# An expert's last 64 second-weight rows by a transfer of their own, nine weight buffers instead of ten

## The chip, the cores and the metric

One core of one Trainium2 chip. The metric is the device time of one execution, in microseconds (us), as a median over runs. All engines, queues and buffers named here are those of this one core.

## What is computed

One layer on 1024 rows of width 256: layer norm with a modulation, attention with 16 heads, a second modulated norm, and a mixture of experts. The second half matters here, cut from the reference:

```python
logits = x @ gate_w.T
weights, sel = top_k(softmax(logits), 4)          # 4 of 60 experts for each row
for each expert e:                                # w13_e: 352 x 256, w2_e: 256 x 176
    gu_e = x @ w13_e.T
    h = silu(gu_e[:, :176]) * gu_e[:, 176:]
    acc = acc + cw_e[:, None] * (h @ w2_e.T)
out = shared + sparse                             # shared: one expert of width 704 for all rows
```

Everything is float32, and the kernel keeps the experts' products in float32.

## The kernel before, in words

**Blocks and pairs.** The kernel sorts the 4 x 1024 choices into blocks of 128 rows. `blocks_of` plans 45 blocks for the 60 experts (the 30 with most rows have a block each, the 30 others share 15 blocks, two to a block with 64 rows each), and a 46th block takes an overflow. Blocks are worked in 23 pairs: pair q has the even block 2q and the odd block 2q+1. All 15 shared blocks are odd ones; their pairs are 1, 2, 4, 5, 7, 8, 10, 11, 13, 14, 16, 17, 19, 20 and 21. So the pattern from pair 3 to pair 20 repeats every three pairs: one pair with two experts, two with three, 8 experts in all. The end differs a little: pair 21 also has three experts, and pair 22 has one and the overflow.

**Weights of an expert.** One row of `in_w` for each of 128 partitions: 2 x 352 values of the first weights, 256 values of the second weights' first 112 rows (`OWN`, on partitions 0 to 111), and 128 values more for the last 64 rows (`REST`): partitions 0 to 63 hold their output columns 0 to 127, partitions 64 to 127 hold columns 128 to 255. That is 1088 values or 4352 B on each partition, 544 KB, in one transfer that SP issues (`load`, L349 to L354) to slot k % 10 of the tile `w` (`RING` = 10). Before it issues load k, SP reads the expert's number (`value_load`) and waits until the block of load k-10 is finished (semaphore `m_y`).

**TensorE's order in pair q** (loop at L1609 and on), with e = 2q: `gate_up` of the even block (x times the first weights, L1567), the first turn of `down_rest` for the two blocks of pair q-2 (L1598), the transposes of rows for the next even block (`rows_of`, L1549), the transposes of the hidden values of pair q-1 (`hidden_T`, L1575 and L1576), the second turn of `down_rest` for pair q-2, `gate_up` of the odd block, `rows_of` again, and `down_own` for pair q-1 (L1582). A `gate_up` waits for all loads of its block and for the rows that ScalarE scales and shifts out of PSUM (`rows_T`, L746, semaphore `m_xtev`).

**The two turns of `down_rest`.** The 64 last hidden values of the even block lie on partitions 0 to 63 and those of the odd block on 64 to 127. In turn 0 each block multiplies its own half of the partitions, which gives one half of the 256 output columns. For the other half of the columns the weights lie on the other partitions, so VectorE copies the hidden values a second time with the halves exchanged (L1106, two copies of 64 x 128 in each pair), and turn 1 uses those. The two blocks' products go to PSUM banks PV and M. Turn 1 waits for turn 0 (`m_half`), and its end raises `m_y`, once for each block.

**VectorE in a pair:** the copies of `hidden_T` (L1106, L1107, L1108), the product of the even block (L1113), the two results of pair q-2 out of PSUM (`result`, L1123, raises `m_yev`, for which `down_own` and GpSimd's scatter wait), the product of the odd block (L1115, L1116). GpSimd issues indirect transfers: gathers of rows (L522), scatters of results (L527). At the end SP reads the scattered results back (L379), and VectorE and GpSimd add them up (L1158, L566).

Of the kernel before, what the change touches and what calls it, by code (L numbers as in the profile page):

```python
# [32 lines left out]
def adaln_layer(nc, x_in, cos_in, sin_in, c_in, wmod_in, wqkv_in, wo_in, wr_in, segu_in, sedn_in,  # L33
                w_in, plan_in, h2rows, ychoice, out):
# [3 lines left out]
    S, D = x_in.shape  # L38
    P = 128
# [16 lines left out]
    I = (w_in.shape[2] - D - D // 2) // (2 * NC)  # L56
# [9 lines left out]
    W_OWN, W_REST = NC * I13, NC * I13 + D  # L66
    WL = W_REST + D // 2
# [14 lines left out]
    RING = 10  # L82
    BUFS = RING
# [31 lines left out]
    with ctx:  # L115
# [34 lines left out]
        w = sb("w", [P, RING, WL])  # L150
# [26 lines left out]
        slotk = sb("slotk", [P, NT * TOPK])  # L177
        row = sb("row", [P, NT * TOPK])
        blk = sb("blk", [P, NT * TOPK])
# [42 lines left out]
        HS, HST = carve(P, 2 * I, 2), carve(P, 4 * P, 2)  # L222
# [27 lines left out]
        ld_w = [sem(f"ld_w{r}") for r in range(RING)]  # L250

        ld_plan, s_plan, s_count, s_look, s_route, m_half = (sem(n) for n in ("ld_plan", "s_plan", "s_count", "s_look", "s_route", "m_half"))
# [72 lines left out]
        def _(sp):  # L325
# [30 lines left out]
            def overflow_weights(b, done):  # L356

                x = sp.value_load(ovei[0:1, bass.ds(b, 1)], min_val=0, max_val=NE - 1)
                sp.dma_start(w[:, 0, :], w_in[bass.ds(x, 1), :, :].rearrange("e p n -> p (e n)")).then_inc(done, 16)
# [5 lines left out]
            sp.wait_ge(m_y, BLOCK_OF[NE - RING] + 1)  # L365
            overflow_weights(0, ld_w[0])

            nov = sp.value_load(novi[0:1, 0:1], min_val=1, max_val=MAXOV)
            with sp.If(nov > 1):
                with sp.Fori(1, nov) as b:  # L370
                    sp.wait_ge(m_yev, b + (NBLK - 1))
                    overflow_weights(b, o_ld)
# [410 lines left out]
        def _(dve):  # L783
# [395 lines left out]
        def _(pe):  # L1179
# [372 lines left out]
            def lanes_of(e):  # L1552
# [3 lines left out]
                return [(k % RING, k // RING + 1, n * i, n) for i, k in enumerate(held)]  # L1556

            alone = [(0, 0, 0, P)]
# [26 lines left out]
            def down_rest(turn, y1, b, blocks):  # L1585
# [136 lines left out]
```

## Time and profile before

| what | us |
|---|---|
| median of 3 runs | 483.09 |
| lowest and highest of the runs | 478.96 and 483.27 |
| the profiled execution's own time | 482.59 |
| its span, first to last instruction | 480.8 |
| mean granted clock of TensorE | 0.954 of full |

The profiled execution's own time is 1.8 us more than its span. Sums below are made against 482.59. The profile names tiles by what shares their memory: QS stands for most of the experts' working buffers, EP, PV and M for PSUM banks, w for the weight ring.

### The profile page before, as it was taken

How to read it: one execution, taken by the hardware profiler on the slowest of the kernel's cores; microseconds unless marked ns; L12 is line 12 of the kernel's file. 1: busy time of each engine (PE TensorE's matmuls, PEld its weight loads, DVE VectorE, ACT ScalarE, POOL GpSimd, SP SyncE). 2: the span in 40 equal slices, each digit the busy share in tenths (PEclk: the TensorE clock that was granted, in tenths of full speed). 3: DMA queues.
4: the chain of work that ended last, by engine and by line, in shares of the span. 5: the costliest groups of instructions: out<-in, count | busy, mean ns of one | idle time of the engine just before them, and what ended most of it. 6: DMA issues, size and time to landing. Idle time of an engine off the chain costs nothing.

```text
span 480.8 us, 7951 instructions
## 1 busy us (share of the span) xinstructions
PE 441.4 (92%) x2866; PEld 214.8 (45%) x2866; DVE 315.2 (66%) x710; ACT 252.1 (52%) x398; POOL 171.5 (36%) x194
## 2 busy tenths in 40 slices
PE   7988999999999999999999699989999999999870
PEld 4554523333333333333566467645555545554450
DVE  7478679999898999953188893534444444444284
ACT  1567657888888888887634132243333333332150
POOL 2058400202032120201010064786565665543343
PEclk8897769999999999999999889999999999999995
DMA  8500000000000000000110661248998998892281
GB/s 270 191 2 1 1 1 1 1 1 2 0 1 1 1 1 2 1 1 0 45 44 1 204 262 41 75 113 280 311 333 299 300 319 286 298 310 90 81 324 55
DMA packets 20530, 54.73 MB, mean 114 GB/s; under 512 B 4513, under 2 KB 8825, under 8 KB 20491
## 3 DMA queue, kind: packets, MB, share of 16 engines
q1 hardware_dynamic: 16075, 45.81, 27.9%
q0 software_dynamic: 4416, 8.41, 5.3%
q8 instruction: 23, 0.38, 0.3%
q14 instruction: 16, 0.13, 0.1%
HBM read 49.74 MB, written 8.13 MB: 120 GB/s over the span
## 4 chain that ended last, share of the span: by engine, by line
PE 75%; DVE 12%; ACT 5%; issue 4%; DMA 3%; SPq 1%; POOL 1%; POOLq 0%; DVEq 0%; ACTq 0%
PE EP L1567 13%; PE PV L1336 13%; PE M L1289 9%; PE EP L1323 6%; PE EP L1326 6%; PE EP L1426 4%; PE EP L1549 3%; PE PV L1582 3%; PE M L1582 3%; PE M L1503 2%; DMA w<-ychoice 2%; PE PV L1598 2%; DVE mx L871 2%; ACT QS L746 2%; PE EP L1254 2%
## 5 line engine op out<-in xcount | busy, mean ns | idle before, releaser
L871 DVE TENSOR_REDUCE mx<-M 128x1 f32<-128x512 f32 x256 | 159.5, 684 | 17.3 <-PE M L1289 17.2
L691 ACT ACTIVATE QS<-EP 128x1024 f32<-128x1024 f32 x128 | 124.1, 1022 | 30.0 <-PE EP L1326 29.6
L1567 PE MATMUL EP<-w,QS 128*128 128x352 f32 (+1 forms) x244 | 65.5, 477 | 5.4 <-ACT QS L746 3.7
L1336 PE MATMUL PV<-QS,VA 128*32 128x512 f32 x512 | 69.0, 612 | 0.0
L1289 PE MATMUL M<-KT,QT 64*128 64x512 bf16 x256 | 61.1, 406 | 3.3 <-DVE mx L871 2.9
L1106 DVE COPY QS<-M 64x128 f32<-64x128 f32 x46 | 13.3, 289 | 70.9 <-PE M L1576 70.6
L741 ACT ACTIVATE OT<-EP 128x176 f32<-128x176 f32 x46 | 14.6, 317 | 74.8 <-PE EP L1567 74.8
L1323 PE MATMUL EP<-QT,KT 64*128 64x512 bf16 x256 | 50.4, 385 | 0.4 <-ACT QS L691 0.2
L1326 PE MATMUL EP<-QTB,xh 34*128 34x512 bf16 x256 | 50.3, 385 | 0.0
L1289 PEld LDWEIGHTS M<-KT,QT 64*128 64x128 bf16 x256 | 18.3, 94 | 66.0 <-DVE mx L871 54.7
L1426 PE MATMUL EP<-segu,QSB 128*128 128x352 f32 x128 | 41.2, 465 | 2.8 <-DVE wide L945 2.8
L746 ACT ACTIVATE QS<-EP,modc 128x128 f32<-128x128 f32 x92 | 37.0, 454 | 10.0 <-PE EP L1549 9.4
L1567 PEld LDWEIGHTS EP<-w,QS 128*128 128x128 f32 (+1 forms) x244 | 28.4, 163 | 29.7 <-issue 12.7
L441 POOL TENSOR_TENSOR rsum<-OT,minus 128x16 f32<-128x16 f32 x6 | 17.5, 2909 | 57.7 <-ACT OT L652 57.7
L527 POOL DMA_INDIRECT ychoice<-xh,tab x26 | 25.7, 987 | 27.9 <-PE EP L1549 12.4
L522 POOL DMA_INDIRECT QS<-h2rows,tab x26 | 28.1, 1082 | 12.6 <-issue 7.6
L1426 PEld LDWEIGHTS EP<-segu,QSB 128*128 128x128 f32 x128 | 23.1, 190 | 15.3 <-issue 3.6
L430 POOL CAST QSB<-negm 128x16 bf16<-128x16 f32 x8 | 2.1, 266 | 69.3 <-DVE negm L880 69.3
L527 POOL DMA_INDIRECT ychoice<-QS,tab x20 | 19.8, 992 | 19.5 <-DVE QS L1123 10.5
L522 POOL DMA_INDIRECT qkv<-h2rows,tab x20 | 20.4, 1022 | 6.1 <-issue 6.1
L1598 PE MATMUL PV<-w,QS 64*64 64x128 f32 (+1 forms) x152 | 20.8, 300 | 0.0
L1598 PE MATMUL M<-w,QS 64*64 64x128 f32 (+1 forms) x152 | 20.8, 300 | 0.0
(277 smaller groups left out, 633.0 us busy)
## 6 DMA issues: line engine op xcount, KB each, us to landing
w<-in_w SPq DMA_DIRECT2D x61, 544.0 KB, 5.6
w<-ychoice SPq DMA_DIRECT2D x8, 512.0 KB, 7.6
segu<-in_segu SPq DMA_DIRECT2D x1, 1408.0 KB, 10.3
x<-in_x SPq DMA_DIRECT2D x2, 512.0 KB, 5.2
wide<-in_wmod SPq DMA_DIRECT2D x1, 1024.0 KB, 7.9
h2rows<-qkv SPq DMA_DIRECT2D x2, 512.0 KB, 3.9
out<-x SPq DMA_DIRECT2D x8, 128.0 KB, 1.8
sedn<-in_sedn SPq DMA_DIRECT2D x1, 640.0 KB, 10.5
```

The costliest lines, as they stand in the source:

```text
L522: pool.indirect_dma_start(out=XG[b], out_offset=None, in_=h2rows, in_offset=bass.IndirectOffsetOnAxis(ap=tab[:, 0, e:e + 1], axis=0), boun ...
L527: pool.indirect_dma_start(out=ychoice, out_offset=bass.IndirectOffsetOnAxis(ap=tab[:, 1, e:e + 1], axis=0), in_=YS[b], in_offset=None, bou ...
L691: nc.scalar.activation(PT[n % 3][:, 2 * p:2 * p + 2, :], EP[p][:, :, :], ACT.Exp, scale=HD ** -0.5).then_inc(e_done, 1)
L746: ins = nc.scalar.activation(XGT[b][:, c * P:(c + 1) * P], BANK[2 + b][:, c * P:(c + 1) * P], ACT.Identity, scale=modc[:, 4, c:c + 1], bia ...
L871: nc.vector.tensor_reduce(out=mx[:, u % 2, q, j, c:c + 1], in_=src, axis=AX.X, op=ALU.max).then_inc(m_free, 1)
L1289: mm(fill(m_free), QT[rows, 2 * g + j // 2, q0:q0 + P], KT[rows, g, 512 * c:512 * c + 512], start=True, stop=True).then_inc(m_fill, 1)
L1323: mm(EP[p][:, i, :], KT[rows, g, keys], QT[rows, 2 * g + p, queries], start=True, stop=False)
L1326: ins = mm(EP[p][:, i, :], KTB[rows, g, keys], QTB[rows, u % 2, p, :], start=False, stop=True)
L1336: ins = mm(PV[HP * j:HP * j + HP, :], VA[:, tt, g, :], PT[n % 3][:, j, :], start=tt == 0, stop=tt == NT - 1)
L1426: ins = mm(EP[part][:, a, 0:SHH], h2T[:, c, t * P:(t + 1) * P], segu[:, c, o:o + SHH], start=c == 0, stop=c == NC - 1)
L1567: ins = mm(BANK[b][lo:lo + n, 0:I13], XGT[b][:, c * P + lo:c * P + lo + n], w[:, r, c * I13:(c + 1) * I13], start=c == 0, stop=c == NC - 1)
L1598: ins = mm(BANK[6 + i][lo:lo + n, cols], HST[b][part, (2 + turn) * P + lo:(2 + turn) * P + lo + n], w[part, r, W_REST:WL], start=False, st ...
```

## The change

- The 128 values for the last 64 rows leave `in_w`: a row has 960 values (3840 B), a transfer 480 KB.
- A new input `in_rest` holds these 64 rows of every expert with all 256 columns. A second transfer for each load brings 64 rows of 1024 B (64 KB) to partitions 0 to 63 for an even block and 64 to 127 for an odd one. Both transfers raise the same semaphore, so that waits count by 32.
- A slot of `w` grows from 1088 to 1216 values for each partition, and the ring has `WRING` = 9 slots: load k waits for the block of load k-9.
- `down_rest` has one turn: each block multiplies its 64 hidden values with all 256 columns. It stands where turn 1 stood. `m_half` goes.
- VectorE's two exchanged copies (L1106) go. `HST` shrinks from 4 to 3 parts, and three small tiles move into the space.

```diff
+    WRING = 9
...
-        w = sb("w", [P, RING, WL])
+        w = sb("w", [P, WRING, WL + D])
...
                 x = sp.value_load(order[0:1, LOADS[k]:LOADS[k] + 1], min_val=0, max_val=NE - 1)
-                if k >= RING:
-                    sp.wait_ge(m_y, BLOCK_OF[k - RING] + 1)
-                sp.dma_start(w[:, k % RING, :], w_in[bass.ds(x, 1), :, :].rearrange("e p n -> p (e n)")).then_inc(ld_w[k % RING], 16)
+                if k >= WRING:
+                    sp.wait_ge(m_y, BLOCK_OF[k - WRING] + 1)
+                weights(x, k % WRING, BLOCK_OF[k] % 2, ld_w[k % WRING])
+
+            def weights(x, r, half, done):
+                rest = slice(HALF * half, HALF * half + REST)
+                sp.dma_start(w[:, r, 0:WL], w_in[bass.ds(x, 1), :, :].rearrange("e p n -> p (e n)")).then_inc(done, 16)
+                sp.dma_start(w[rest, r, WL:WL + D], rest_in[bass.ds(x * REST, REST), :]).then_inc(done, 16)
...
-                for i in range(experts):
-                    here, there = slice(REST * i, REST * i + REST), slice(REST * (1 - i), REST * (1 - i) + REST)
-                    nc.vector.tensor_copy(HST[b][there, 3 * P:4 * P], H[here, 2 * P:3 * P])
...
-                        pe.wait_ge(ld_w[r], 16 * loads)
+                        pe.wait_ge(ld_w[r], 32 * loads)
...
-                    d = (i + turn) % 2
-                    part, cols = slice(HALF * d, HALF * d + HALF), slice(P * d, P * d + P)
+                    part = slice(HALF * i, HALF * i + REST)
                     for r, loads, lo, n in lanes:
-                        ins = mm(BANK[6 + i][lo:lo + n, cols], HST[b][part, (2 + turn) * P + lo:(2 + turn) * P + lo + n], w[part, r, W_REST:WL],
-                                 start=False, stop=turn == 1)
-                    ins.then_inc(m_y if turn else m_half, 1)
+                        ins = mm(BANK[6 + i][lo:lo + n, 0:D], HST[b][part, 2 * P + lo:2 * P + lo + n], w[part, r, WL:WL + D],
+                                 start=False, stop=True)
+                    ins.then_inc(m_y, 1)
...
                 gate_up(e + 1, 0, lanes_of(e))
-                if q >= 2:
-                    down_rest(0, e - 2, b, two(e - 4))
                 if q:
                     rows_of(e + 1)
                     hidden_T(e, 1 - b)
                 if q >= 2:
-                    down_rest(1, e - 2, b, two(e - 4))
+                    down_rest(b, two(e - 4))
...
             down_own(NBLK // 2, 1 - b, two(NBLK - 2))
-            down_rest(0, NBLK, 1 - b, two(NBLK - 2))
+            down_rest(1 - b, two(NBLK - 2))
             shared_half(EARLY, 1, 1).then_inc(s_up, 1)
-            down_rest(1, NBLK, 1 - b, two(NBLK - 2))
```

## Rows read from the trace of the kernel before

**Rows 1.** The page: busy time by engine, and the last-ended chain's shares.
```profile
PE 441.4 (92%) x2866; PEld 214.8 (45%) x2866; DVE 315.2 (66%) x710; ACT 252.1 (52%) x398; POOL 171.5 (36%) x194
...
PE 75%; DVE 12%; ACT 5%; issue 4%; DMA 3%; SPq 1%; POOL 1%; POOLq 0%; DVEq 0%; ACTq 0%
```

**Rows 2.** Busy time by stretch: three pairs, from one odd gate_up to another.
```profile
core 0: us, PE busy (x) PEld busy (x) DVE busy (x) ACT busy (x) POOL busy (x), PEclk, DMA share, GB/s
416.21:433.97 17.76, 17.23 (x109) 9.05 (x109) 7.54 (x28) 6.65 (x18) 6.93 (x7) 1.00 0.87 289
```

**Rows 3.** Timeline of TensorE, from an even gate_up to the next odd one.
```profile
365.80 1.45 PE L1567 MATMUL EP<-w,QS 128*128 128x352 f32 x4
367.18 0.33 PE L1598 MATMUL PV<-w,QS 64*64 64x128 f32 x2
...
367.56 0.44 PE L1549 MATMUL EP<-ident,QS 128*128 128x128 f32 x2
367.84 0.38 PE L1575 MATMUL M<-ident,QS 128*112 128x128 f32 x2
...
368.26 0.33 PE L1598 MATMUL PV<-w,QS 64*64 64x128 f32 x2
368.27 0.33 PE L1598 MATMUL M<-w,QS 64*64 64x128 f32 x2
368.42 0.28 PE L1598 MATMUL PV<-w,QS 64*64 64x128 f32 x2
...
368.90 0.52 PE L1567 MATMUL EP<-w,QS 128*64 128x352 f32 x2 [0.19 <-ACT QS L746]
```

**Rows 4.** Timeline of ScalarE in the same stretch.
```profile
368.04 0.81 ACT L746 ACTIVATE QS<-EP,modc 128x128 f32<-128x128 f32 x2 [0.43 <-PE EP L1549]
```

**Rows 5.** SP's waits.
```profile
SPq L354 <- PE M L1598: 94.9, 19, 42.3
```

**Rows 6.** Timeline of the end of the last pair.
```profile
445.71 0.70 PE L1582 MATMUL PV<-w,QS 112*128 112x256 f32 x2 [0.22 <-DVE QS L1123]
...
446.77 0.37 PE L1598 MATMUL PV<-w,QS 64*128 64x128 f32 x1
...
447.38 0.98 POOL L527 DMA_INDIRECT ychoice<-QS,tab  x1 [0.31 <-issue]
...
448.79 0.27 PE L1598 MATMUL PV<-w,QS 64*128 64x128 f32 x1
...
449.10 0.42 DVE L1123 TENSOR_TENSOR xh<-PV,MOD 128x256 f32<-128x256 f32 x1 [3.44 <-PE M L1598]
...
450.30 0.97 POOL L527 DMA_INDIRECT ychoice<-xh,tab  x1 [1.94 <-DVE xh L1123]
```

**Rows 7.** Line L1106, VectorE's exchanged copies, over the whole span.
```profile
L1106 DVE COPY QS<-M x46: 283/289/294, 315.1 to 444.1; 64x128 f32<-64x128 f32 x46
```

**Rows 8.** Line L354, weight loads: two loads after the release at 416.
```profile
L354 SPq DMA_DIRECT2D w<-in_w x1: 341/341/341, 416.2 to 416.2; - x1
DMA to landing us min/median/max: 4.4/4.4/4.4
...
L354 SPq DMA_DIRECT2D w<-in_w x1: 333/333/333, 417.3 to 417.3; - x1
DMA to landing us min/median/max: 5.4/5.4/5.4
```

**Rows 9.** The same line at 368.9: first and second load after that release.
```profile
L354 SPq DMA_DIRECT2D w<-in_w x1: 342/342/342, 368.9 to 368.9; - x1
...
L354 SPq DMA_DIRECT2D w<-in_w x1: 333/333/333, 370.3 to 370.3; - x1
DMA to landing us min/median/max: 5.6/5.6/5.6
```

**Rows 10.** The page's DMA issues: KB of each, median us to landing.
```profile
w<-in_w SPq DMA_DIRECT2D x61, 544.0 KB, 5.6
...
out<-x SPq DMA_DIRECT2D x8, 128.0 KB, 1.8
```

More of the change, by code:

```diff
@@ L33, in adaln_layer @@
 def adaln_layer(nc, x_in, cos_in, sin_in, c_in, wmod_in, wqkv_in, wo_in, wr_in, segu_in, sedn_in,
-                w_in, plan_in, h2rows, ychoice, out):
+                w_in, rest_in, plan_in, h2rows, ychoice, out):
     f32, bf16, i32, u32 = mybir.dt.float32, mybir.dt.bfloat16, mybir.dt.int32, mybir.dt.uint32
@@ L221, in adaln_layer @@
         YS = carve(P, D, 4) + [xhf[:, D * b:D * b + D] for b in range(BUFS - 4)]
-        HS, HST = carve(P, 2 * I, 2), carve(P, 4 * P, 2)
+        HS, HST = carve(P, 2 * I, 2), carve(P, 3 * P, 2)
+        slotk, row, blk = carve(P, NT * TOPK, 3)
         SL = [OT[:, I * b:I * b + I] for b in range(2)]
@@ L249, in adaln_layer @@
         ld_qkv, ld_wo, ld_wr, ld_sh = sem("ld_qkv"), sem("ld_wo"), sem("ld_wr"), sem("ld_sh")
-        ld_w = [sem(f"ld_w{r}") for r in range(RING)]
-        ld_plan, s_plan, s_count, s_look, s_route, m_half = (sem(n) for n in ("ld_plan", "s_plan", "s_count", "s_look", "s_route", "m_half"))
+        ld_w = [sem(f"ld_w{r}") for r in range(WRING)]
+        ld_plan, s_plan, s_count, s_look, s_route = (sem(n) for n in ("ld_plan", "s_plan", "s_count", "s_look", "s_route"))
         s_eq, s_one, s_lo, s_hi, s_cells, s_read, s_tab = (sem(n) for n in ("s_eq", "s_one", "s_lo", "s_hi", "s_cells", "s_read", "s_tab"))
@@ L364, in _ @@
             sp.wait_ge(s_over, 1)
-            sp.wait_ge(m_y, BLOCK_OF[NE - RING] + 1)
-            overflow_weights(0, ld_w[0])
+            sp.wait_ge(m_y, BLOCK_OF[NE - WRING] + 1)
+            overflow_weights(0, SPARE % 2, ld_w[NE % WRING])
             nov = sp.value_load(novi[0:1, 0:1], min_val=1, max_val=MAXOV)
@@ L1555, in lanes_of @@
                 n = P // len(held)
-                return [(k % RING, k // RING + 1, n * i, n) for i, k in enumerate(held)]
-            alone = [(0, 0, 0, P)]
+                return [(k % WRING, k // WRING + 1, n * i, n) for i, k in enumerate(held)]
+            alone = [(NE % WRING, 0, 0, P)]
             def gate_up(e1, b, lanes):
@@ L1583, in down_own, with down_rest @@
                            start=True, stop=False)
-            def down_rest(turn, y1, b, blocks):
-                if turn:
-                    pe.wait_ge(m_half, y1)
+            def down_rest(b, blocks):
                 parts = max(len(lanes) for lanes in blocks)
@@ L1633, in _ @@
             b = (NBLK // 2) % 2
-            down_rest(0, NBLK - 2, b, two(NBLK - 4))
             hidden_T(NBLK, 1 - b)
-            down_rest(1, NBLK - 2, b, two(NBLK - 4))
+            down_rest(b, two(NBLK - 4))
             shared_half(EARLY, 1, 0)
@@ L1655, in _ @@
                     down_own(i + NBLK // 2, b, [alone])
-                    for turn in range(2):
-                        down_rest(turn, i + NBLK, b, [alone])
+                    down_rest(b, [alone])
                 pe.wait_ge(m_yev, nov + (NBLK - 1))
@@ L1698 @@
     w2 = a["ffn_w2"].transpose(0, 2, 1)
-    row = np.zeros((E, P, NC * I2 + D + D // 2), np.float32)
+    row = np.zeros((E, P, NC * I2 + D), np.float32)
     row[:, :, 0:NC * I2] = a["ffn_w13"].reshape(E, I2, NC, P).transpose(0, 3, 2, 1).reshape(E, P, NC * I2)
-    row[:, 0:own, NC * I2:NC * I2 + D] = w2[:, 0:own]
-    row[:, 0:rest, NC * I2 + D:] = w2[:, own:I, 0:D // 2]
-    row[:, rest:2 * rest, NC * I2 + D:] = w2[:, own:I, D // 2:D]
+    row[:, 0:own, NC * I2:] = w2[:, 0:own]
     arrays["w"] = row
+    arrays["rest"] = w2[:, own:I].reshape(E * rest, D)
     plan = np.zeros((E, 5), np.float32)
```

17 lines of the change are left out of this document (7 added, 10 removed).

## The prediction

> **What bounds the kernel now.** First the page: TensorE is busy 92% of the span, and three quarters of the chain that ended last are its own [rows 1]. The reader is to see that work taken from TensorE's queue can shorten the kernel, and that VectorE's copies alone can't. Next the busy time by stretch. Three pairs, from one odd gate_up to the one three pairs on, take 17.76 us, or 5.92 for a pair; TensorE is busy 17.23 of them at the full granted clock (1.00, which is 2.4 GHz), and the 16 DMA engines are busy for 0.87 of the time [rows 2]. So there are two near bounds, and the change touches both. Then the timeline of one half pair [rows 3]: turn 0 of down_rest starts at 367.18 and rows_of at 367.56, so the turn holds TensorE for 0.38 us; hidden_T follows at 367.84, turn 1 at 368.26 to 368.70, and the odd gate_up starts at 368.90 after 0.19 idle. That idle ends with ScalarE, whose two activations for the gate_up run from 368.04 for 0.81 us [rows 4]. The chain is therefore rows_of, ScalarE, gate_up, and turn 1 lies beside it, while turn 0 lies in it. Last, SP's queue: its loads wait for TensorE's L1598, 19 times and 94.9 us in all [rows 5], so SP often stands ready and issues when a slot comes free. The list of waits has no line in which TensorE waits for a transfer to w: the loads are in time today.
>
> **Part by part: what goes.** Turn 0 goes from the chain: 0.38 us in a pair. What comes next is still ScalarE: rows_of to gate_up stays at 368.90 - 367.56 = 1.34. TensorE's own work in it grows. A turn is two rounds on 128 columns in 0.44; two rounds on 256 columns (L1582) take 0.70 [rows 6]. So the new down_rest ends 0.70 + 0.70 = 1.40 after rows_of starts, of which the last tenth or so is the pipeline's tail that the next gate_up may overlap. Both ends are near 1.34; I take the ScalarE bound, with 0 to 0.2 lost on it as the range. A pair without a stall is then 5.92 - 0.4 = 5.5 us, and 21 pairs (2 to 22) save 21 x 0.4 = 8.4. Both blocks' matmuls still start 0.01 us apart on the two halves of the array [rows 3], so I expect them side by side as before.
>
> VectorE's two copies go, 0.29 us each [rows 7]. In the pairs they are nearly free of price, since VectorE is busy only 7.54 of 17.76 us [rows 2]; where down_own waits for VectorE's results it is some 0.2 us, and I leave it out except at the end. There the wait is 0.22 [rows 6]. At the end more goes: today the last turn 1 ends at 448.79 + 0.27 = 449.06, because a piece of the shared expert lies between the turns. With one turn right behind down_own (446.77 + 0.7 = 447.45), and down_own itself 0.6 earlier (turn 0 of the block before, and the copies), the last m_y comes at about 446.8, 2.2 us earlier. The scatter behind it, at 450.30, can't start before the one at 447.38 is issued (0.98, and 0.31 idle), 448.07 if that is 0.6 earlier: also 2.2. The chain goes on through this scatter, so 2.2 count. Gains: 8.4 + 2.2 = 10.6.
>
> **What is added: less lead for the loads.** With ten slots a load waits for the block ten loads back, with nine for the one nine back. Counting the plan out: pair q's down_rest now frees, in a pair before a shared odd block, first the two loads of the odd block of pair q+1, then the even block of q+2. With ten slots the first of those two had been freed a pair earlier. So the second load of a shared block must be issued and landed between the end of down_rest in one pair and the odd gate_up in the next, which is one pair, 5.5 us. How long does it take now? After the release at 416.2 the second load is issued at 417.3 and lands 5.4 later: 6.5 us after the first issue [rows 8]. After that at 368.9 it is 370.3 + 5.6 - 368.9 = 7.0 [rows 9]. Mean 6.7. It will not be in time. This is the wait that the change adds: TensorE stands at the odd gate_up, and down_own, the next pair and the next release stand behind it.
>
> To 6.7 comes the price of the second transfers. SP issues one more instruction for each load (a bulk issue is 0.33 us), so second loads are issued some 0.5 later; but the first load's data is still moving then, so I hide that. The bytes are the same, 480 + 64 = 544 KB. Bounds of a 64 KB transfer in the queue: below, 0 or a gain, as the bulk transfer is 64 KB shorter; above, 1.8 us, what a whole 128 KB store takes by itself to landing [rows 10], if nothing of it overlapped. Two loads follow each other at 2.1 us though each takes over 4 [rows 8], so overlap is the rule, and I take the low end, 0.1 each: 6.9.
>
> The rows show no transfer to half the partitions in this stage. The Trainium skill (SBUF — State Buffer, "Door 1: The DMA port swizzle") says that partitions 0 to 63 reach only 8 of the 16 ports, with an asymptote of 218 GB/s: 64 KB would take 0.30 us instead of the 0.15 of all 16 ports (436 GB/s there). By that estimate the second load would land 0.3 later, and the time would be near 485; no run here shows it yet.
>
> How often does it stall? Say the release in pair q is at 0. The odd gate_up of q+1 starts at 6.9 instead of 5.5, 1.4 late. The next release (in q+1) comes before that gate_up and isn't late, so the second load of q+2, if that is shared too, lands at 5.5 + 6.9 = 12.4; but TensorE gets there only at 6.9 + 5.5 = 12.4 as well. So of two shared pairs in a row the second is free. Three in a row (19, 20, 21) stall twice. Pairs 4, 7, 10, 13, 16, 19 and 21 stall: 7 x 1.4 = 9.8. At the end the even block of pair 22 is freed a pair later than before, in pair 21. Odd to even gate_up is 5.92 - 3.10 = 2.82 [rows 3], so it is wanted 1.4 + 2.8 = 4.2 after that release and lands some 4.8 after it (4.4 [rows 8], the small transfer, and the issue): 0.6. Losses: 10.4.
>
> **Sum:** 482.59 (profiled execution) - 10.6 + 10.4 = 482.4. The median of the runs is 0.5 above the profiled execution, so 482.9: no change that can be measured. About 1% is what a measurement of this kernel can tell from none.
>
> **Rivals.** (1) The nine slots suffice. The DMA engines are idle for 0.13 of the time [rows 2] and a pair before a single-expert block brings only two loads, so the second load may meet an empty queue and land at 6.0 or sooner. Against it: after the release at 416.2 the first load landed in a quick 4.4, and the second still needed 6.5 [rows 8]. Stalls of 0 to 0.5 in seven pairs give 472.5 to 476.5; as a point 475. (2) The other side: the small transfers cost. If each of them holds the queue for 0.6 us rather than 0.1 (64 rows of 1024 B on half the partitions, and another completion), the second load lands at 7.9, the seven stalls are 2.4 each, the one at the end 1.2: 482.9 - 10.4 + 18.0 = 490.5. It decides from 0.45 each (0.7 later in seven pairs is 4.9 us). For it: a share of 0.87 [rows 2] leaves the DMA engines little room. (3) The change doesn't shorten TensorE's half pair as it says: with 1.40 to 1.55 between rows_of and gate_up a pair saves 0.2 only. In the 14 pairs where no load is late that is 2.8 lost, 485.7.
>
> **Chances.** Forecast 0.45, rival 1 0.22, rival 2 0.25, rival 3 0.08. For the forecast alone the second load's landing between 6.4 and 7.5 gives 479 to 487. The range reaches into both sides: 476 to 490.5. Faster by over 1% (below 478.3) is rival 1 and a little of the forecast, 0.25; slower (above 487.9) is most of rival 2 and a little of the others, 0.28; between, 0.47.
>
> **What would show it.** In the trace after: no turn 0, rows_of right behind the even gate_up (right: 0.38 earlier). Odd gate_ups with two loads that wait for a DMA on w, about 1.4 us, in one pair of three, and 5.5 us for the pairs between; three pairs then take 17.7. SP issues each load in two, some 1.6 us apart from one load to the next instead of 1.1. The last results of VectorE come about 2.2 us sooner after the last odd gate_up. The forecast is wrong if TensorE never waits for w (rival 1), if the second load lands over 7.5 us after the first issue (rival 2), or if gate_up stands behind down_rest and not behind ScalarE (rival 3).

## The result, and the profile after

The changed kernel takes 486.88 us (median of 20 runs, 482.21 to 490.97), the kernel before 481.92 in as many runs beside it: a ratio of 1.010, interval 1.007 to 1.013. The ratio leaves out the runs over 1.5% above the fastest of their kernel, one of 684.25 us of the kernel before among them. So it is slower by 1.0%, where I had forecast no change that can be measured. Its profiled execution took 488.72 us with a span of 486.9.

Page of the changed kernel: busy time, the chain's shares, gate_up's group, and the DMA issues.
```profile
PE 434.9 (89%) x2714; PEld 215.3 (44%) x2714; DVE 301.5 (62%) x664; ACT 250.2 (51%) x398; POOL 170.9 (35%) x194
...
q1 hardware_dynamic: 20955, 45.82, 29.0%
...
PE 65%; DVE 13%; DMA 7%; SPq 6%; issue 4%; ACT 3%; POOL 1%; DVEq 0%; ACTq 0%; POOLq 0%
...
L1569 PE MATMUL EP<-w,QS 128*128 128x352 f32 (+1 forms) x244 | 68.2, 501 | 21.3 <-DMA w<-in_rest 19.5
...
w<-in_w SPq DMA_DIRECT2D x61, 480.0 KB, 4.1
...
w<-in_rest SPq DMA_DIRECT2D x61, 64.0 KB, 4.6
```
TensorE has 152 matmuls and 6.5 us of busy time less than in [rows 1]; its share of the chain fell from 75% to 65%, and DMA and SP's queue, 3% and 1% before, have 7% and 6%. The new item is the 19.5 us in which gate_up (L1569) waits for `in_rest`. The list of waits gives their number, 14, and the longest, 2.5 us; and SP waits for slots 14 times and 64.2 us, where it was 19 and 94.9 [rows 5]:

Waits of TensorE and of SP in the changed kernel (engine, line, what it waited for: us in all, times, longest).
```profile
PE EP L1569 <- DMA w<-in_rest: 19.5, 14, 2.5
...
SPq L358 <- PE M L1597: 64.2, 14, 36.5
```

Windows of the changed kernel: the stage from the first odd gate_up to the last, two groups of three pairs, one pair without a stall.
```profile
core 0: us, PE busy (x) PEld busy (x) DVE busy (x) ACT busy (x) POOL busy (x), PEclk, DMA share, GB/s
310.09:449.17 139.08, 117.76 (x644) 64.53 (x642) 41.92 (x153) 46.90 (x133) 78.14 (x76) 0.96 0.81 258
365.03:384.57 19.54, 15.70 (x89) 8.65 (x90) 5.62 (x21) 6.35 (x18) 12.07 (x12) 1.00 0.89 294
403.91:422.97 19.06, 17.07 (x94) 9.48 (x90) 5.81 (x22) 6.35 (x18) 11.12 (x11) 0.91 0.81 256
398.62:403.91 5.29, 5.29 (x33) 2.71 (x34) 0.93 (x4) 2.15 (x6) 3.03 (x3) 1.00 0.83 273
```
And the same stage in the kernel before.
```profile
310.56:439.94 129.38, 124.01 (x783) 65.27 (x782) 53.37 (x192) 49.03 (x133) 78.33 (x76) 1.00 0.82 273
```
The stage grew by 9.7 us. It is one first pair of 5.04 and seven groups of three pairs: before (129.38 - 5.04) / 7 = 17.76 a group, after 19.15. What takes the 9.7 down to the 6.1 us between the two spans is a start 0.5 earlier and an end 3.1 shorter (last odd gate_up to the end of the span: 480.8 - 439.94 = 40.9, and 486.9 - 449.17 = 37.7). A pair without a stall takes 5.29 instead of 5.92, and TensorE is busy in all of it.

Timeline of TensorE in the changed kernel, even to odd gate_up, in a pair without a stall.
```profile
420.40 1.45 PE L1569 MATMUL EP<-w,QS 128*128 128x352 f32 x4
421.69 0.38 PE L1551 MATMUL EP<-ident,qkv 128*128 128x128 f32 x2
421.91 0.38 PE L1577 MATMUL M<-ident,QS 128*112 128x128 f32 x2
422.12 0.27 PE L1578 MATMUL M<-ident,QS 128*128 128x128 f32 x1
422.33 0.43 PE L1597 MATMUL PV<-w,QS 64*64 64x256 f32 x2
...
422.97 0.56 PE L1569 MATMUL EP<-w,QS 128*128 128x352 f32 x1
```
Set beside [rows 3]: turn 0 is gone and rows_of (L1551) starts 1.29 us after the even gate_up instead of 1.76, so the turn had cost 0.47, not its own 0.38. From rows_of to the odd gate_up it is 1.28 instead of 1.34, and no wait for ScalarE is printed before this gate_up (over the whole span such waits were 3.7 us in 18 places, and are 0.6 in one): TensorE's own work now fills that time.

Timelines of TensorE around three odd gate_ups (pairs 7, 10 and 16) of the changed kernel.
```profile
352.95 2.19 PE L1569 MATMUL EP<-w,QS 128*64 128x352 f32 x8 [2.40 <-DMA w<-in_rest]
...
372.28 1.40 PE L1569 MATMUL EP<-w,QS 128*64 128x352 f32 x8 [2.07 <-DMA w<-in_rest]
...
411.11 2.31 PE L1569 MATMUL EP<-w,QS 128*64 128x352 f32 x8 [1.99 <-DMA w<-in_rest]
```
TensorE finishes down_rest, stands, and starts the moment the second load has landed. The stalls at the odd gate_ups are 2.55, 2.40, 2.07, 1.63, 1.99, 2.12 and 1.10 in the pairs I had named (4, 7, 10, 13, 16, 19, 21), 1.69, 1.21 and 0.90 in pairs 11, 14 and 20, where I had expected none, and 0.68 in pair 22; three more waits are 0.77 or less.

Timeline of SP's queue in the changed kernel, after the release at 364.9.
```profile
365.05 0.34 SPq L358 DMA_DIRECT2D w<-in_w  x1
365.58 0.48 SPq L359 DMA_DIRECT2D w<-in_rest  x1
366.83 0.34 SPq L358 DMA_DIRECT2D w<-in_w  x1
...
369.03 0.34 SPq L358 DMA_DIRECT2D w<-in_w  x1
...
370.82 0.34 SPq L358 DMA_DIRECT2D w<-in_w  x1
...
372.60 0.34 SPq L358 DMA_DIRECT2D w<-in_w  x1
```
SP needs 1.78 us for a load (365.05 to 366.83) instead of 1.1 to 1.4 [rows 8, rows 9]. The two loads of pair 10 are issued at 365.05 and 366.83, and the gate_up that needs both starts at 372.28, 7.2 after the first issue. Those of pair 11 could have been issued at 370.2, when the next release came, but SP was still busy with the load before; they go out at 370.82 and 372.60. After the wait that ended at 364.9 these five loads follow one another without another wait.

One more thing shows. The granted clock falls to half (0.5 of full, the 1.2 GHz level) for 3.4 us behind the stalls of pairs 4, 7 and 16, but not behind those of pairs 10 and 19 (2.07 and 2.12), which were as long as that of pair 16. A window from an odd gate_up to the next even one is 1.4 us longer then:

Windows of the changed kernel, odd to even gate_up (pairs 7, 10, 16).
```profile
352.95:357.06 4.11, 4.11 (x14) 2.37 (x15) 0.40 (x2) 1.12 (x3) 2.17 (x3) 0.58 1.03 354
372.28:374.99 2.71, 2.63 (x14) 1.41 (x15) 0.40 (x2) 1.12 (x3) 2.10 (x3) 1.00 0.96 312
411.11:415.22 4.11, 4.11 (x15) 2.40 (x16) 0.40 (x2) 1.12 (x3) 3.19 (x4) 0.58 1.00 343
```
Yet a group of three pairs with such a fall isn't longer (19.67, 19.69 and 19.06 for pairs 4 to 6, 7 to 9 and 16 to 18, against 19.54 and 19.34 for the two without): in pairs 5, 8 and 17 the slow clock stands in place of the second stall that pairs 11, 14 and 20 have. So the loads' pace sets the group, as far as five groups of one trace can show it, and TensorE's slow work lies inside it.

### The profile page after: what moved, and what is told of

Same layout as the page of the kernel before. It is cut to its first block, busy times and chain, and to the rows that moved or that the text cites. A ratio compares the mean times of both kernels' runs of the same rounds, so it can differ in the third digit from the quotient of the medians.

```text
span 486.9 us, 7784 instructions
## 1 busy us (share of the span) xinstructions
PE 434.9 (89%) x2714; PEld 215.3 (44%) x2714; DVE 301.5 (62%) x664; ACT 250.2 (51%) x398; POOL 170.9 (35%) x194
## 4 chain that ended last, share of the span: by engine, by line
PE 65%; DVE 13%; DMA 7%; SPq 6%; issue 4%; ACT 3%; POOL 1%; DVEq 0%; ACTq 0%; POOLq 0%
PE PV L1338 13%; PE M L1291 9%; PE EP L1569 8%; DMA w<-in_rest 7%; PE EP L1325 6%; PE EP L1328 6%; PE EP L1428 5%; SPq L359 2%; SPq L358 2%; DVE mx L876 2%; PE EP L1256 2%; SPq L350 2%; PE PV L1597 2%; DVE x L1160 2%; PE EP L1551 1%
## 5 line engine op out<-in xcount | busy, mean ns | idle before, releaser
L1569 PE MATMUL EP<-w,QS 128*128 128x352 f32 (+1 forms) x244 | 68.2, 501 | 21.3 <-DMA w<-in_rest 19.5
L746 ACT ACTIVATE OT<-EP 128x176 f32<-128x176 f32 x46 | 14.6, 317 | 95.2 <-PE EP L1569 95.2
L1569 PEld LDWEIGHTS EP<-w,QS 128*128 128x128 f32 (+1 forms) x244 | 30.1, 168 | 49.4 <-issue 28.1
L1109 DVE COPY QS<-M 128x128 f32<-128x128 f32 x23 | 6.7, 291 | 57.8 <-PE M L1578 57.8
L446 POOL TENSOR_TENSOR rsum<-OT,minus 128x16 f32<-128x16 f32 x6 | 17.4, 2908 | 57.7 <-ACT OT L657 57.7
L1117 DVE TENSOR_TENSOR QS<-OT,EP 128x64 f32<-128x64 f32 x23 | 5.1, 221 | 41.1 <-ACT OT L746 41.1
L532 POOL DMA_INDIRECT ychoice<-QS,tab x20 | 19.8, 989 | 24.0 <-DVE QS L1125 20.2
L523 POOL TENSOR_TENSOR qkv<-hT,iotaf 128x1248 bf16<-128x1248 bf16 x2 | 8.4, 4222 | 32.1 <-DVE hT L1060 32.1
```

The source lines that it names most:

```text
L446: pool.tensor_tensor(rsum[:, u % 2], o[:, :, :, HD], minus1[:, 0:16].rearrange("p (t j) -> p t j", t=4), ALU.pow).then_inc(s_rsum, 1)
L532: pool.indirect_dma_start(out=ychoice, out_offset=bass.IndirectOffsetOnAxis(ap=tab[:, 1, e:e + 1], axis=0), in_=YS[b], in_offset=None, bou ...
L1569: ins = mm(BANK[b][lo:lo + n, 0:I13], XGT[b][:, c * P + lo:c * P + lo + n], w[:, r, c * I13:(c + 1) * I13], start=c == 0, stop=c == NC - 1)
```

## The experiments

Theory: the stall comes from a slot being given back too late for nine slots. Rivals: the second transfer and its issue do it; or the DMA queue's throughput does, whatever the slots are. In three of the five groups of runs the kernel before itself took 490 to 496 us (480 and 481 in the other two), and the traces read there show ScalarE idle for some microseconds where the profile names nothing in the kernel that holds it. I call those runs disturbed: their totals aren't compared, only stretches free of such idle times. Lengths of the stage are from the first odd gate_up to the last.

### Slots, transfers and bytes one at a time

**e1, the changed kernel with ten slots:**
```diff
-    WRING = 9
+    WRING = 10
```


> The changed kernel with ten weight slots instead of nine, nothing else. Theory A (the loss is the shorter lead of the loads): a pair without a stall took 5.28 us in the changed kernel, so with the old lead the odd gate_ups hardly wait for w; the time falls to the median of before minus about 10, some 472 us (469 to 476). Rival B (the loss is the second transfer itself, its issue and its half of the partitions): the stalls stay, 482 to 487 us.

472.11 us against 479.92 of the kernel before beside it, ratio 0.979 (0.969 to 0.989); stage 124.61; a group of three pairs has one wait, now in its second shared pair (5, 8, 11, 14, 17 and 20).

Waits of TensorE and two windows (the stage; three pairs), changed kernel with ten slots.
```profile
PE EP L1569 <- DMA w<-in_rest: 8.9, 7, 2.0
...
310.22:434.83 124.61, 113.58 (x644) 61.97 (x642) 41.27 (x150) 47.01 (x133) 78.17 (x76) 1.00 0.87 284
...
343.67:360.97 17.30, 15.71 (x93) 8.58 (x89) 5.81 (x22) 6.36 (x18) 11.15 (x11) 1.00 0.95 321
```
So the tenth slot alone is worth 14.5 us of the stage (139.08 - 124.61), and the other parts of the change are a gain of 2%. The tenth slot fits beside them: this kernel differs in nothing but `WRING`. Waits are left even so: with shorter pairs, ten slots are short too.

**e2, the kernel before with nine slots** (`WRING` = 9; its last load goes to slot 6 instead of 0):
```diff
-        w = sb("w", [P, RING, WL])
+        w = sb("w", [P, WRING, WL])
...
-                if k >= RING:
-                    sp.wait_ge(m_y, BLOCK_OF[k - RING] + 1)
+                if k >= WRING:
+                    sp.wait_ge(m_y, BLOCK_OF[k - WRING] + 1)
```


> The kernel before (two turns, one transfer of 544 KB) with nine weight slots. Theory A: the second load of a shared block lands 6.7 us after its release against a pair of 5.92, so seven odd gate_ups stall some 0.8 us, and one even gate_up at the end about 1; 5 to 7 us over the kernel before, 487 to 489 us. Rival B: the lead costs nothing by itself, within 1 us of the kernel before.

486.4 us against 479.92, ratio 1.011 (1.002 to 1.021); the difference of the medians, 6.5, is in the 5 to 7 expected.

Waits of TensorE and the stage's window, kernel before with nine slots.
```profile
PE EP L1568 <- DMA w<-in_w: 10.7, 11, 1.6
...
305.73:443.31 137.58, 122.88 (x783) 65.90 (x782) 53.34 (x192) 48.92 (x133) 78.13 (x76) 1.00 0.78 261
```
The stage grows by 8.2 (137.58 - 129.38) with one transfer of 544 KB, both turns and all copies in place. Its 137.6 is also nearly the 139.1 of the changed kernel, though that one has 5 us less of TensorE's busy time in the stage (122.88 and 117.76): with nine slots the gain is given back as longer waits (10.7 and 19.5).

**e3, the changed kernel with ten slots and one transfer,** the last 64 rows on both halves of the partitions (608 KB a load):
```diff
-                sp.dma_start(w[:, r, 0:WL], w_in[bass.ds(x, 1), :, :].rearrange("e p n -> p (e n)")).then_inc(done, 16)
-                sp.dma_start(w[rest, r, WL:WL + D], rest_in[bass.ds(x * REST, REST), :]).then_inc(done, 16)
+                sp.dma_start(w[:, r, :], w_in[bass.ds(x, 1), :, :].rearrange("e p n -> p (e n)")).then_inc(done, 16)
```


> One turn and ten slots, but one transfer for an expert: the last 64 rows with all 256 columns stand in both halves of the partitions, so a load has 608 KB instead of 544, and SP issues once. Theory A with the DMA engines as next bound: 8 loads of 12% more bytes in three pairs ask for about 17 us where TensorE needs 15.8; 477 to 482 us, and slower than the run with two transfers and ten slots. Rival B: without the second transfer's issue and half partitions it is the fastest of all, 470 to 474 us.

469.76 us, ratio 0.976 (0.966 to 0.985); stage 122.28; waits of gate_up for w 6.5 us in 9 places. The expected 477 to 482 fails: with 12% more bytes in the queue, moved at 316 GB/s over the stage, it is no slower than e1, so the queue's throughput wasn't the bound at e1's 284. What the bytes cost by themselves isn't shown, since SP's second issue went at the same time. The intervals of this run and of e1 overlap.

**e4, the kernel before with its load cut in 480 and 64 KB,** both to all partitions:
```diff
-                sp.dma_start(w[:, k % RING, :], w_in[bass.ds(x, 1), :, :].rearrange("e p n -> p (e n)")).then_inc(ld_w[k % RING], 16)
+                sp.dma_start(w[:, k % RING, 0:W_REST], w_in[bass.ds(x, 1), :, 0:W_REST].rearrange("e p n -> p (e n)")).then_inc(ld_w[k % RING], 16)
+                sp.dma_start(w[:, k % RING, W_REST:WL], w_in[bass.ds(x, 1), :, W_REST:WL].rearrange("e p n -> p (e n)")).then_inc(ld_w[k % RING], 16)
```


> The kernel before (two turns, ten slots) with each load as two transfers of the same bytes, 480 KB and 64 KB (128 partitions x 512 B). Theory A: SP needs some 1.7 us for a load instead of 1.1, and the loads that have 0.1 to 0.4 us to spare today come late a few times; 0 to 3 us over the kernel before, 482 to 485 us. Rival B (a second transfer holds the queue 0.6 us or more each time): 8 of them in three pairs are 4.8 us, 490 us or more.

481.24 us, ratio 1.001 (0.997 to 1.005): with ten slots and the long pairs a second transfer costs nothing that can be measured. (Here its 64 KB go to all partitions, in the changed kernel to half of them.)

SP's wait for slots, and the page's queue and DMA issues, kernel before with the load cut in two.
```profile
SPq L354 <- PE M L1600: 64.9, 19, 37.2
...
q1 hardware_dynamic: 24859, 45.82, 28.9%
...
w<-in_w SPq DMA_DIRECT2D x61, 64.0 KB, 4.8
```
SP still waits 19 times for a slot, in all 30 us less than in [rows 5]: the second issues use up time in which SP stood ready.

### The order of the turns and the copies

**e6, e10 and e15, the kernel before with turn 0 behind hidden_T** instead of ahead of rows_of:
```diff
-                if q >= 2:
-                    down_rest(0, e - 2, b, two(e - 4))
                 if q:
                     rows_of(e + 1)
                     hidden_T(e, 1 - b)
                 if q >= 2:
+                    down_rest(0, e - 2, b, two(e - 4))
                     down_rest(1, e - 2, b, two(e - 4))
```


> The kernel before with one line moved: turn 0 of down_rest stands behind hidden_T, right ahead of turn 1. Theory A (turn 0 cost because it stood in the chain rows_of, ScalarE, gate_up): from rows_of to the odd gate_up TensorE then needs 0.70 + 0.44 + 0.44 = 1.6 us instead of 1.34, and turn 0's 0.47 ahead of rows_of is gone: 0.2 us for a pair, 3 to 5 us less than before. Rival B (it is the amount of work alone): no change within 1 us.

> The kernel of e6_before_turn_0_later again: the kernel before (ten slots, one 544 KB transfer, both copies of the exchanged blocks) with turn 0 done behind the hidden transposes of the own block. Theory A (the order of the turns is worth something by itself, by hiding the wait of TensorE on the activation): 3 to 5 us less than before, 475 to 477. Theory B (all the gain of a pair is in the dropped copies and the half block): no change against before, ratio within 1 per cent of 1.

> The kernel before with turn 0 behind the hidden transposes of the own block. In a call with the kernel before at 480 to 483: theory A (the order is worth something by itself) 475 to 477; theory B (all the gain of a pair is in the half block and the dropped copies) ratio within 1 per cent of 1.

500.86, 506.48 and 503.74 us, with the kernel before at 490.01, 495.54 and 492.9: all disturbed, no total to be had. **e7 and e11, the changed kernel at ten slots with the two exchanged copies back,** fared the same (501.03 and 513.1 us, the kernel before at 490.01 and 495.54):
```diff
-        HS, HST = carve(P, 2 * I, 2), carve(P, 3 * P, 2)
+        HS, HST = carve(P, 2 * I, 2), carve(P, 4 * P, 2)
...
+                for i in range(experts):
+                    here, there = slice(REST * i, REST * i + REST), slice(REST * (1 - i), REST * (1 - i) + REST)
+                    nc.vector.tensor_copy(HST[b][there, 3 * P:4 * P], H[here, 2 * P:3 * P])
```


> The changed kernel with ten slots, but VectorE still makes its two exchanged copies in each pair, which nobody reads. Theory A (TensorE's queue and the loads are the bound, VectorE's copies were nearly free): within 2 us of the ten-slot kernel, 471 to 475 us; at most the wait of down_own for the results comes back, 0.2 us in some pairs. Rival B (the copies were worth 0.58 us in each pair): 13 us more, 484 us.

> The kernel of e7_ten_slots_copies_kept again: the changed kernel at ten slots with the two copies of the exchanged blocks put back beside it. Theory A (copies lie beside TensorE's work and cost it little): 471 to 475, as with ten slots alone. Theory B (the gain of ten slots comes from the copies' going): the time is back near that of before, 478 to 484.

The last two pairs are free of stalls and of strange idle times, so windows over those two pairs can be set side by side. They repeat: 11.18 in e6, e10 and e15, 10.72 in e7 and e11. The kernel before:
```profile
428.01:439.94 11.93, 11.54 (x82) 5.59 (x83) 5.02 (x19) 4.50 (x12) 3.90 (x4) 1.00 0.61 219
```
Turn 0 later (e10):
```profile
454.45:465.63 11.18, 10.95 (x85) 5.72 (x83) 4.97 (x19) 4.29 (x12) 3.89 (x4) 1.00 0.69 262
```
Ten slots with the copies kept (e7):
```profile
445.48:456.20 10.72, 10.72 (x66) 5.38 (x66) 4.10 (x15) 4.30 (x12) 3.90 (x4) 1.00 0.73 245
```
Ten slots without them (e1):
```profile
424.24:434.83 10.59, 10.59 (x67) 5.40 (x67) 2.88 (x11) 4.31 (x12) 3.89 (x4) 1.00 0.78 246
```
By half of each difference, the order of the turns is worth 0.38 us a pair, the two rounds in place of four 0.23, and the copies 0.07: together 0.67. So theory A holds for a pair in both, though the order is worth nearly twice the 0.2 that I had expected of it. The kernels' totals show neither, since all five runs were disturbed.

### One transfer with nine slots

**e5, e12, e16 and e18, nine slots and one transfer of 608 KB** (the edit of e3 without the tenth slot):

> One turn, nine slots, one transfer of 608 KB for an expert instead of 480 + 64 KB. Against the changed kernel it takes away SP's second issue (a load every 1.1 us instead of 1.8) and nothing of the short lead. Theory A (lead first, SP's issues second): the second load of a shared block is issued 0.7 us sooner, so the ten late gate_ups shrink by some 0.7 each; 478 to 483 us, still 8 us or more over the same kernel with ten slots. Rival B (SP's second issue makes the stalls): near the ten-slot kernel, 470 to 474 us.

> The kernel of e5_one_transfer_nine_slots again: nine slots, one padded transfer of 608 KB in place of 480 and 64 KB. Theory A (with nine slots the stalls come from the slot's late release, and the second issue of SP and the second landing add part): the stalls sum to some 11 us instead of 19.5, time 478 to 483. Theory B (the two issues are all of the stall): few stalls left, 470 to 474.

> Nine slots and one padded transfer of 608 KB. In a call with the kernel before at 480 to 483: theory A (the late release stalls, the second issue of SP adds part) 478 to 483, sum of the waits for w some 11 us; theory B (the two issues are all of the stall) 470 to 474.

> Nine slots, one padded transfer of 608 KB, as e5, e12 and e16. Theory A (the late release stalls, the second issue and landing add part): waits for w of 11 us or so in 9 to 12 places, against 19.5 in 14; in a call with the kernel before at 480 to 483 a time of 478 to 483. Theory B (the two issues are all of the stall): few waits, 470 to 474.

The first three are disturbed (494.54, 503.22 and 505.68 us, the kernel before at 490.01, 495.54 and 492.9). The fourth is not: 484.79 us beside 481.0, ratio 1.010 (1.002 to 1.018). That is a miss for both theories: nothing like 470 to 474, but also not the 478 to 483 that I had given theory A.

Waits of TensorE and three windows (the stage; three pairs without and three with a fall of the clock), one transfer with nine slots, fourth run.
```profile
PE EP L1567 <- DMA w<-in_w: 16.8, 10, 2.7
...
306.21:445.38 139.17, 120.67 (x643) 66.44 (x641) 41.18 (x150) 46.88 (x133) 78.14 (x76) 0.94 0.81 282
...
360.82:379.33 18.51, 15.73 (x93) 8.67 (x90) 5.80 (x22) 6.35 (x18) 11.97 (x12) 1.00 0.96 342
379.33:399.11 19.78, 17.07 (x93) 9.44 (x90) 5.80 (x22) 6.34 (x18) 10.34 (x11) 0.91 0.82 287
```
The stage, 139.17, is that of the changed kernel, but it is made up in another way. Its clock fell five times behind stalls (pairs 4, 7, 13, 19 and 21), in the changed kernel three times. Of the five groups of pairs 4 to 18 the two without a fall took 18.51 and 18.11, where the changed kernel's two took 19.54 and 19.34: there the second transfer and its issue cost 1.1 us a group, net of what 12% more bytes cost here. The stalls of pairs 11 and 17 are 0.86 and 0.50 in those groups, the changed kernel's second stalls 1.69 and 1.21. The groups with a fall took 19.3 to 19.8 here and 19.1 to 19.7 there. So without the second transfer the loads come sooner and the five groups are 1.9 shorter in all, but the first stall of a group stays (1.3 to 2.7 us), and the last four pairs, with two falls of the clock, are 2.0 longer (28.16 and 26.20) and take the gain.

### The slot given back earlier

**e8, e9, e14 and e17, two rings in place of one:** ten slots for the 480 KB, given back after down_own (a new semaphore `m_own`), and eight for the 64 KB, issued four loads behind; gate_up waits for the first, down_rest for the second (`N1` = 10, `BEHIND` = 4; `late_rest` waits for `m_y` of the block eight loads back):
```diff
-                if k >= WRING:
-                    sp.wait_ge(m_y, BLOCK_OF[k - WRING] + 1)
-                weights(x, k % WRING, BLOCK_OF[k] % 2, ld_w[k % WRING])
+                if k >= N1:
+                    sp.wait_ge(m_own, BLOCK_OF[k - N1] + 1)
+                bulk(held[k], k % N1, ld_w[k % N1])
+                if k >= BEHIND:
+                    late_rest(k - BEHIND)
```


> A version meant to beat both: one turn, two transfers of 480 and 64 KB, but rings of their own in the same space as ten full slots: ten slots for the bulk, free again after down_own (2.6 us sooner than after down_rest), eight for the last 64 rows, issued four loads behind the bulk; gate_up waits for the bulk alone. Theory A (the lead is all that is missing): no late gate_up, 22 pairs of 5.28 us, 8 us under the ten-slot kernel, 463 to 467 us. Rival B (the DMA engines or SP are the bound once the ring is no longer): within 3 us of the ten-slot kernel, 469 to 473 us.

> The kernel of e8_rings_apart again, on another call, since the runs of the kernel before were themselves 10 us longer than usual beside e8. Two rings: ten slots for the bulk of every expert's weights, whose slot comes free after the first weights' last use of the turn (down_own), and eight for the last 64 rows. Theory A (the load waits for a free slot, and the slot's hand-out is what limits the stage): no wait for weights is left, the stage from the first to the last odd gate_up is 22 pairs and a half of 5.3 us, about 117 to 120 us against 124.6 with ten slots in one ring, and the time is 463 to 467. Theory B (the queue's throughput limits the stage, whatever the slots do): the loads come no earlier, stage 122 to 125, time 469 to 473.

> Two rings, ten slots freed after the first weights' last use for the bulk, eight for the last 64 rows. In a call with the kernel before at 480 to 483: theory A (the slot's late release is what stalls) no wait for weights, stage from the first to the last odd gate_up 117 to 120 us, time 463 to 467; theory B (the queue's throughput limits the stage) stage 122 to 125, time 469 to 473.

> Two rings, as e8, e9 and e14: ten slots, freed after down_own, for the bulk, eight for the last 64 rows. In the three calls before, ScalarE stood idle for 2 to 5 us behind a finished gate_up at about the same five places of the stage, which is 30 us of the time and in all kernels of those calls; outside those places the pairs took 5.18 to 5.29 us and TensorE never waited for weights. Theory A (the slot's late release is what stalls): the same again, and in a call with the kernel before at 480 to 483 a stage of 117 to 120 us and a time of 463 to 467. Theory B (the queue's throughput limits the stage as soon as nothing else does): in such a call waits for the bulk appear, stage 122 to 125, time 469 to 473.

Three were disturbed (496.39, 506.43 and 504.41 us, the kernel before at 490.01, 495.54 and 492.9). The fourth gave 464.89 us beside 481.0, ratio 0.965 (0.956 to 0.974), and beats both kernels.

Waits of TensorE, two windows (the stage; three pairs) and the page's DMA issues, rings apart, fourth run.
```profile
PE EP L1584 <- DMA w<-in_w: 2.7, 4, 1.1
...
310.25:428.62 118.37, 113.43 (x643) 61.84 (x641) 41.18 (x150) 46.89 (x133) 78.10 (x76) 1.00 0.92 301
...
391.07:406.79 15.72, 15.64 (x93) 8.50 (x90) 5.80 (x22) 6.34 (x18) 11.12 (x11) 1.00 1.02 330
...
w<-in_w SPq DMA_DIRECT2D x61, 480.0 KB, 7.5
```
The same 61 loads in two transfers each, through the same queue, in a stage of 118.4 us instead of 139.1, at 301 GB/s instead of 258. A transfer takes 7.5 us to land and not 4.1, and TensorE hardly waits for it, since it is issued early enough. That speaks for the theory and rules out both rivals as the bound: the queue can do this pace, and two transfers a load don't prevent it. How much of the gain is the earlier release alone isn't shown, because this kernel changes three more things against the changed one: a tenth slot for the 480 KB (14.5 us of the stage by e1), a gate_up that no longer waits for the 64 KB, and their issue four loads later. Against e1 the stage is 6.2 shorter (124.61 and 118.37). The waits aren't quite gone: 2.7 us in four places, where I had expected none. And in the three disturbed groups this kernel was slower than the kernel before, by 1.5 to 1.9% (ratios 1.015, 1.019 and 1.018).

### Were the disturbed runs the kernels' doing?

**e13, the kernel of e1 again,** in the fourth group of runs:

> The kernel of e1_ten_slots again (ratio 0.979 there), beside e14 to e16. In the last two calls the runs of the kernel before were themselves 8 to 14 us longer, and all kernels tried there came out above it. Theory A (the core stood still for reasons outside the kernels in those calls, and more so in kernels that run closer to the edge): in a call in which the kernel before takes 480 to 483, this one takes 470 to 474 again; in a call in which it takes 490 or more, this one shows the same unexplained idle times too and is no faster. Theory B (those four kernels are slow by their own doing): this one is 2 per cent faster than before in every call.

504.24 us, where it had taken 472.11; the kernel before 492.9. So the same kernel takes 32 us more in a disturbed group, and the kernel before 13 more: the disturbance isn't one kernel's doing, but it took more from the one that was faster. Line L746, ScalarE's first activation behind each gate_up, of the undisturbed run (e1):
```profile
L746 ACT ACTIVATE OT<-EP x46: 317/318/319, 310.4 to 436.3; 128x176 f32<-128x176 f32 x46
...
  PE EP L1569: 81.3, 46
```
The same line of the same kernel in the disturbed run (e13):
```profile
L746 ACT ACTIVATE OT<-EP x46: 317/317/318, 311.1 to 470.1; 128x176 f32<-128x176 f32 x46
...
  PE EP L1569: 62.1, 29
  remote: 27.3, 6
  issue: 20.6, 11
```
In e1 all 46 waits end with gate_up; in e13 17 of them end with nothing that the profile can name, and six of these hold 27.3 us. What it was stays open.

## Why the prediction was wrong

**What held.** The mechanism and its place: the second load of a shared block comes late, TensorE stands at the odd gate_up of pairs 4, 7, 10, 13, 16, 19 and 21, and little else that is new (1.8 us in four places, 0.6 of it forecast). The pairs between are shorter, and the end is. Two sizes and one step failed.

**The sum, closed.** On the profiled executions the gains are 14.3 us in the pairs and 3.1 at the end, 17.4 where I had 10.6. The losses are 19.5 of waits and 3 x 1.4 = 4.2 at the slow clock, 23.7 where I had 10.4: the seven stalls 13.9 for 9.8, the second stalls and the slow clock 3.8 + 4.2 = 8.0 for nothing, the other waits 1.8 for 0.6. That leaves 6.3, and the spans differ by 6.1. So an error of 6.8 on one side and one of 13.3 on the other cancel by half. That the 486.88 lies inside the range of 476 to 490.5, and 4 us from the point, is luck in part: the terms weren't right.

**"A pair without a stall is then 5.92 - 0.4 = 5.5."** It is 5.29 or less; three such pairs take 15.72 (e17) and not 16.5, a gain of 0.68 a pair where I took 0.4. Turn 0 was priced by its distance to rows_of (0.38), but taking it out brought rows_of 0.47 forward; 0.06 more came between rows_of and gate_up, and 0.07 from the copies, which I left out; the last 0.08 of the 0.68 I can't assign. Over 21 pairs that is 14.3 us instead of 8.4. The step also harmed the next one: a shorter pair makes each stall longer by as much.

**"1.4 late."** The stalls of the seven pairs are 2.0 in the mean (13.86 / 7). In pair 10: the release is at 364.9, the first issue 0.2 later, which I had left out; 7.1 to the second landing, where I took 6.9; 0.1 to the start; and the pair is 0.2 shorter than I took. 1.4 + 0.2 + 0.2 + 0.1 + 0.2 = 2.1, and 2.07 was measured. The landing itself was priced well: in the seven pairs the second load is there 6.5 to 7.4 after the first issue, 7.0 in the mean.

**"So of two shared pairs in a row the second is free."** This is the step that turned the sign. I let the second release start a fresh transfer, "isn't late", with the 6.9 us of a quiet queue. But SP needs 1.78 us a load, eight loads in three pairs are 14.2 us of its time, and at the second release it was still issuing: the last load of pair 11 went out 2.4 us after the release at 370.2, and took 6.5 more to land where that of pair 10 had taken 5.3. So it was there 8.9 after the release and not 6.9; about half of the 2.0 is the later issue (I had rested on 1.1 to 1.4) and half the longer landing (on 5.4 to 5.6). Pair 14 is alike (2.4 and 6.3). Pairs 11, 14 and 20 stall for 0.9 to 1.7, and in pairs 5, 8 and 17 the slow clock covers the same: together the 8.0 us that the sum had at nothing. Take them out of the sum, and the changed kernel is 1.9 faster than the kernel before. I had written "second loads are issued some 0.5 later; but the first load's data is still moving then, so I hide that". For one hand-out that is so (e4: nothing with ten slots); for hand-outs that run into one another it costs 1.1 a group (e18).

**The group as a whole.** I forecast 17.7 us for three pairs after the change; in pairs 4 to 18 it is 19.46 in the mean ((422.97 - 325.67) / 5). The runs give a shorter way to that number. With R slots and eight loads in a group of T, a slot is used again every T x R / 8. By the same five groups that is 21.9 us in the changed kernel, 21.5 with one transfer (e18: 19.08 a group), 21.3 in the kernel before with nine slots (e2: 18.91), 21.7 in the changed one with ten (e1: 17.37), and 21.2 with one transfer and ten (e3: 16.99). Of these kernels only the one before, at 17.76 x 10 / 8 = 22.2, had no wait. So in five kernels a slot came round in 21.2 to 21.9 us, and with 21.6 a group takes 21.6 x 8 / 9 = 19.2 where TensorE's work is 15.7. This is worked out after the fact, from kernels that wait, and their waits are in it; from the kernel before, which doesn't wait, the number can't be read. With 19.2 the five groups come out 7.2 longer than before. They are 8.5 longer; the pairs ahead of them are 1.3 shorter and the four behind them 2.5 longer, and that makes the stage's 9.7.

**The end.** 2.2 us was forecast and 3.1 measured. VectorE's last results came 2.75 sooner behind the last odd gate_up (6.75 and not 9.50), which is the cause that I gave, one turn right behind down_own. The other 0.4 is within what the end varies by: in e4, with the order of the kernel before, it is 39.55 and not 40.9.

**The rivals.** Rival 1 (nine slots suffice) fell with e2. Rival 2 had the sign, and its 490.5 is near, but not by its mechanism, that each small transfer holds the queue for 0.6 us: that would be 4.8 a group, e4 shows none of it with ten slots, and against e18 it is 1.1. Its sign, a second load that lands over 7.5 after the first issue, did show in pairs 11 and 14 (8.3 and 8.1), but not in the seven pairs that stall first. The share of the queue's packets rose from 27.9% of 480.8 us to 29.0% of 486.9, that is by 7.1 us in the mean of the 16 engines, 0.12 a load; I had taken 0.1. Rival 3 fell as to the time: gate_up follows rows_of in 1.28, sooner than before. Its sign did show, though: gate_up stands behind down_rest and not behind ScalarE, as TensorE's work there took 1.28 and not the 1.40 that I had added up.

**The port rule.** The 64 KB to half the partitions landed in 4.6 us in the changed kernel, 5.3 with ten slots and 6.9 with the rings apart, and 64 KB to all of them in 4.8 (e4, where they were issued 0.5 behind the bulk as well). The Trainium skill (SBUF — State Buffer, "Door 1: The DMA port swizzle") gives partitions 0 to 63 half of the ports, from which the prediction had estimated 0.15 us more for 64 KB. The landings move by far more than that with the traffic beside them, so no run here shows the rule or refutes it.

**Never weighed:** that a stall can halve the clock. In the changed kernel it made no group longer, since the loads were the bound; the one-transfer version had two more falls in its last four pairs and lost there what it had gained.

## What to carry to other kernels

For a ring of buffers work out how long a slot is taken, from the issue of its load to its release and the next issue, and compare that, times loads over slots, with the time of the work: while the first is longer, work saved only becomes waiting (here 14 us of it), and slots decide. The tenth slot was worth 14.5 us of 139 with the short pairs, and 8.2 of 138 with the long ones. Price a load by what its issuer does in a row, not alone, when hand-outs can run into one another. And before adding or saving slots ask what holds each one longest: the kernel that gives the large part back one step earlier, and has ten slots for it, is 22 us below the changed kernel and 7 below e1, with as many transfers.

The Trainium skill has the general rule (DMA: Bandwidth & Descriptors, "Rules for kernel authors"): issue a transfer early, wait for it late, and its fixed cost lies beside the work. The run with the rings apart agrees: its transfers take 7.5 us to landing instead of 4.1, and the kernel 22 us less.

## What the hardware showed that I had not expected

- Stalls of 1.9 to 2.7 us are sometimes followed, sometimes not, by 3.4 us at half the clock: after 1.99 yes, after 2.07 and 2.12 no, and after 2.0 with ten slots no; in e18 after 1.92 yes. Each time in the changed kernel gate_up takes 2.2 to 2.6 us instead of 1.40, and the stretch to the next gate_up 4.11 instead of 2.71.
- With ten slots 608 KB a load made the kernel no slower than 480 + 64 (e3 and e1): the DMA engines moved 316 GB/s over the stage where they had moved 273 at a busy share of 0.82 in the kernel before, and 342 over three pairs of e18. The busy share of 0.87 that I had read as little room did not mean a full queue: with the rings apart it went to 1.02 over three pairs.
- In three of five groups of runs ScalarE started up to 5 us late behind finished matmuls. The same kernel was 0.979 of the kernel before in an undisturbed group and 1.018 in a disturbed one (e1, e13).
